# Graph network kernel, gated pass: the two edge-term columns made stationary, in four column groups

## What is computed

```
# layer 1: gated messages
msg_in = concatenate([h[src], h[dst], e64], axis=-1)
messages = (silu(msg_in @ w1 + b1) @ w2 + b2) * sigmoid(msg_in @ wg + bg)
agg = segment_sum(messages, dst) / max(deg, 1)
...
# layer 3, rounds 1 and 2: attention over edges
a_e = edge_attr_128 @ We @ att_e          # the edge term: one number an edge and round
alpha = leaky_relu(a_s[src] + a_d[dst] + a_e, 0.2)
```

## Time and profile before

| | us |
|---|---|
| median of 3 runs | 1996.36 |
| lowest, highest | 1994.1, 1997.79 |
| span of the profiled execution | 1993.2 |
| PE busy / weight loads busy | 1706.9 / 1412.5 |
| DVE / ACT / POOL busy | 1396.3 / 913.6 / 982.6 |

### The profile page before, as it was taken

The page is one execution under the profiler, slowest core; times in us unless marked ns, Lnnn a source line. Parts: engine busy times, 40 slices in busy tenths (PEclk is TensorE's granted clock), DMA queues, the critical chain, the costliest instruction groups (busy, mean ns, idle before and its releaser), DMA issues. The chain is left out here.

```text
span 1993.2 us, 43518 instructions
## 1 busy us (share of the span) xinstructions
PE 1706.9 (86%) x13678; PEld 1412.5 (71%) x13678; DVE 1396.3 (70%) x4290; ACT 913.6 (46%) x2490; POOL 982.6 (49%) x1002
## 2 busy tenths in 40 slices
PE   6799999999999749998649998956599989399996
PEld 5699999999998715556547886756478768166664
DVE  5677888888887698996667765556777654745556
ACT  2566676776776366773305553420255433411100
POOL 3766677777776120000557777735677774300000
PEclk9799999999999759999659999976699999699998
DMA  6887788888877002332532111117121111345442
GB/s 193 252 249 239 231 252 243 249 252 255 254 240 230 10 5 84 128 123 112 174 91 66 43 43 42 49 61 185 43 66 42 41 44 37 121 176 202 175 166 89
DMA packets 149677, 276.91 MB, mean 139 GB/s; under 512 B 28807, under 2 KB 88845, under 8 KB 147188
## 3 DMA queue, kind: packets, MB, share of 16 engines
q1 hardware_dynamic: 109134, 191.58, 29.5%
q0 software_dynamic: 35456, 79.88, 14.3%
q10 hardware_dynamic: 4854, 2.55, 0.5%
HBM read 228.82 MB, written 45.08 MB: 137 GB/s over the span
## 5 line engine op out<-in xcount | busy, mean ns | idle before, releaser
L972 POOL DMA_INDIRECT gated_rows<-p_tab,src_idx x416 | 429.0, 1031 | 176.4 <-issue 102.2
L1364 POOL DMA_INDIRECT ring<-table,src_idx x384 | 382.9, 997 | 145.3 <-issue 89.3
L2194 PE MATMUL bank<-counts,mean_xs 128*128 128x416 bf16 (+2 forms) x1350 | 220.1, 322 | 32.1 <-DVE mean_xs L1696 32.1
L1013 PE MATMUL bank<-gated_wide_q,gated_comb 128*128 128x256 f32 x832 | 218.6, 386 | 0.0
L1170 DVE TENSOR_TENSOR gated_pre<-bank,gated_rows 128x512 f32<-128x512 f32 x208 | 142.8, 687 | 105.1 <-PE bank L1013 103.0
L1496 ACT COPY attention_counts<-bank 128x475 f32 (+1 forms) x224 | 127.6, 570 | 183.7 <-PE bank L1523 179.9
L2194 PEld LDWEIGHTS bank<-counts,mean_xs 128*128 128x128 bf16 x1350 | 126.3, 98 | 116.6 <-issue 35.1
L1086 ACT ACTIVATE gated_sig<-gated_pre 128x512 f32<-128x512 f32 x208 | 131.2, 631 | 155.3 <-DVE gated_pre L1170 153.3
L1534 PE MATMUL bank<-attention_counts,h_sb 128*128 128x232 f32 (+1 forms) x900 | 193.3, 342 | 0.5 <-issue 0.5
L1534 PEld LDWEIGHTS bank<-attention_counts,h_sb 128*128 128x128 f32 x900 | 159.2, 192 | 28.3 <-issue 1.5
L1519 PE MATMUL bank<-attention_wide_a,scratch 128*128 128x300 f32 x448 | 161.1, 442 | 12.2 <-DVE scratch L1577 11.2
(11 more groups left out here) (440 smaller groups left out, 3985.9 us busy)
## 6 DMA issues: line engine op xcount, KB each, us to landing
counts<-count_tabs SPq DMA_DIRECT2D x16, 2675.0 KB, 9.9
h_sb<-in_edge_attr_dram SPq DMA_DIRECT2D x51, 512.0 KB, 4.9
count_tabs<-mean_counts SPq DMA_DIRECT2D x40, 535.0 KB, 2.7
gated_relr<-rel_rows SPq DMA_DIRECT2D x104, 128.0 KB
gated_ids<-id_rows SPq DMA_DIRECT2D x26, 512.0 KB
gated_wide_q<-q_tab SPq DMA_DIRECT2D x208, 64.0 KB
attend_hot_lo<-low_hots SPq DMA_DIRECT2D x52, 256.0 KB
gated_ea<-in_edge_attr_dram SPq DMA_DIRECT2D x51, 256.0 KB
```

The costliest lines, as they stand in the source:

```text
L972: pool.indirect_dma_start(out=rows[:, q % TICKS, c, :], out_offset=None, in_=p_tab, in_offset=bass.IndirectOffsetOnAxis(ap=src_idx[:, b, j ...
L1013: mm = pe.matmul(PRE[q % 2][:, c * 2 * P:(c + 1) * 2 * P], comb[:, u, k, c, :], wide_q[:, u, c, :], start=True, stop=True)
L1364: pool.indirect_dma_start(out=rows[:, n % RING, j, :], out_offset=None, in_=table, in_offset=bass.IndirectOffsetOnAxis(ap=src_idx[:, gathe ...
L2194: mm = pe.matmul(BANKS_D[q % ND][:, 0:width], xs[l][:, m // 3, m % 3, :], counts[:, s % 2, m // 3, at:at + width], start=(m == 0), stop=(m ...
```

## The change

The edge terms are made once a batch instead of once a step. `ae_v` becomes 32 columns wide, the last 30 of them zero, and is the stationary operand; the turned attributes of one chunk are the moving one, 128 columns. Each of the four chunks of a batch has its own group of 32 columns of the array: chunk j writes the PSUM partitions 32 j to 32 j + 31 of ST, and rows 32 j and 32 j + 1 are the two terms of its 128 edges, one row a round. The four products stand ahead of the silu transposes of the batch's second step (k = 1); the first step has none.

ACT copies the 128 x 128 result once a batch to `ae_rows`, ahead of the silu copy. SP stores rows l, 32 + l, 64 + l, 96 + l of four batches at a time in the DRAM tensor `edge_terms` (`keep_edge_terms`, two transfers for four batches). `attend` loads its round's rows with two transfers into `ae_jp`, and DVE rearranges them to `ae_e`; the transposes L2443 are gone. `place_eaT` waits for one more step of ST, since `eaT` is now read one step longer. Two semaphores for `ae_rows` and one for its placing are added to the 35 that the pass clears at its end.

```
+            ae_rows = sb("ae_rows", [P, 2, AG_, P])
...
+                    def keep_edge_terms(g):
+                        sp.wait_ge(ae_placed, (g + 1) * AG_)
+                        for l in range(2):
+                            sp.dma_start(edge_terms[l, g * AG_:(g + 1) * AG_, :, :].rearrange("b j p -> j b p"),
+                                         ae_rows[l:P:AE_COLS, g % 2, :, :]).then_inc(ae_kept[g % 2], 16)
...
+                            if b % AG_ == 0 and b >= 2 * AG_:
+                                keep_edge_terms(b // AG_ - 2)
...
                     def turn_silu(q):
                         pe.wait_ge(silu_ready, q + 1)
                         reach(pe, sT_ready, q)
+                        _, k, _ = batch(q)
+                        if k == PAIRS - 1:
+                            for j in range(J):
+                                pe.matmul(ST[j * AE_COLS:(j + 1) * AE_COLS, 2 * P:3 * P], ae_v[:, :], eaT[:, (q - k + j // 2) % TRN, j % 2, :],
+                                          start=True, stop=True, skip_group_check=True)
                         for c in range(2):
-                            pe.transpose(ST[:, c * P:(c + 1) * P], silu[:, q % 2, c, :], ident[:, :])
-                        for c in range(2):
-                            mm = pe.matmul(ST[:, 2 * (P + c):2 * (P + c) + 2], eaT[:, q % TRN, c, :], ae_v[:, :], start=True, stop=True)
+                            mm = pe.transpose(ST[:, c * P:(c + 1) * P], silu[:, q % 2, c, :], ident[:, :])
                         mm.then_inc(s_turned, 1)
...
-                        reach(act, s_turned, q - TRN + 1)
+                        reach(act, s_turned, q - TRN + 2)
...
-                        act.copy(ae[:, :, b, 2 * k:2 * k + 2], ST[:, 2 * P:2 * P + 4].rearrange("p (c l) -> p l c", l=2))
+                        if k == PAIRS - 1:
+                            reach(act, ae_kept[b // AG_ % 2], 32 * (b // AG_ // 2))
+                            act.copy(ae_rows[:, b // AG_ % 2, b % AG_, :], ST[:, 2 * P:3 * P]).then_inc(ae_placed, 1)
...
+                    even = NB // 16 * 16
+                    for rows_ in (slice(0, even), slice(even, NB)):
+                        sp.dma_start(ae_jp[rows_, :], edge_terms[l - 1, rows_, :, :].rearrange("b j p -> b (j p)")).then_inc(ae_loaded, 16)
...
-                        if g == AE_AT - 1:
-                            for j in range(J):
-                                mm = pe.transpose(A_SRC[0:NB, j * P:(j + 1) * P], ae[:, l - 1, :, j], ident[:, :])
-                            mm.then_inc(ae_turned, 1)
...
                         if g == AE_AT:
-                            dve.wait_ge(ae_turned, 1)
-                            link(dve.tensor_copy(ae_e[:, :].rearrange("b (p j) -> b j p", j=J), A_SRC[0:NB, :].rearrange("b (j p) -> b j p", p=P)))
+                            dve.wait_ge(ae_loaded, 32)
+                            link(dve.tensor_copy(ae_e[:, :].rearrange("b (p j) -> b j p", j=J), ae_jp[:, :].rearrange("b (j p) -> b j p", p=P)))
```

More of the change, by code:

```diff
@@ L163, in build_program @@
     place_a, origin_a = sb("place_a", [1, NSB * AROW], I32), sb("origin_a", [1, LAST], I32)
-    ae_v, ae = sb("ae_v", [P, 2]), sb("ae", [P, 2, NB, J])
+    AE_COLS = 32
+    ae_v = sb("ae_v", [P, AE_COLS])
     w_tab, w_c = sb("w_tab", [P, NB, J]), sb("w_c", [P, NB, J])
@@ L198, in build_program @@
     aux_rows = dram("aux_rows", [NB * BE, 4])
+    edge_terms = dram("edge_terms", [2, NB, J, P])
     tables = [dram(f"table{i}", [NODES, P]) for i in range(5)]
@@ L843, in gated_pass @@
             we_g, we_T, ae_c = sb("we_g", [P, 2, P]), sb("we_T", [P, 2, P]), sb("ae_c", [P, 2])
-            ae_in, ae_turned, ae_taken, ae_made = [sem(n) for n in ("ae_in", "ae_turned", "ae_taken", "ae_made")]
+            ae_in, ae_turned, ae_taken, ae_made, ae_blank = [sem(n) for n in ("ae_in", "ae_turned", "ae_taken", "ae_made", "ae_blank")]
+            AG_ = 4
+            ae_rows = sb("ae_rows", [P, 2, AG_, P])
+            ae_placed, ae_kept = sem("ae_placed"), [sem(f"ae_kept{i}") for i in range(2)]
             rows = sb("rows", [P, TICKS, 2, 2 * P])
@@ L867, in gated_pass @@
             SELF_AT = {16 + 8 * g: g for g in range(NG)}
-            per_round = [*self_sems, *ids_in, *looks_kept, looks_made, *ea64_in, *ea128_in, *relr_in, *q_in, ea_turned, made, s_turned, m_made, summed, eaT_ready, sig_ready, sT_ready,
+            per_round = [*self_sems, ae_placed, *ae_kept, *ids_in, *looks_kept, looks_made, *ea64_in, *ea128_in, *relr_in, *q_in, ea_turned, made, s_turned, m_made, summed, eaT_ready, sig_ready, sT_ready,
                          hot_b_ready, pre_ready, silu_ready, msg_ready, hot_ready, hotT_ready, added]
@@ L955, in _ @@
                             keep_looks(g)
+                        for g in range(NB // AG_ - 2, NB // AG_):
+                            keep_edge_terms(g)
+                        for u in range(2):
+                            sp.wait_ge(ae_kept[u], 32 * (NB // AG_ // 2))
                         for u in range(2):
@@ L1108, in _ @@
                     act.wait_ge(ae_made, 1)
-                    act.copy(ae_v[:, :], bank[7][:, 2 * P:4 * P:P]).then_inc(ae_taken, 1)
+                    act.wait_ge(ae_blank, 1)
+                    act.copy(ae_v[:, 0:2], bank[7][:, 2 * P:4 * P:P]).then_inc(ae_taken, 1)
                     with rounds_of(act) as rr:
@@ L1130, in _ @@
                     dve.memset(ones_b[:, :], 1.0).then_inc(ready, 1)
+                    dve.memset(ae_v[:, :], 0.0).then_inc(ae_blank, 1)
                     dve.wait_ge(loaded, 16 * 6)
@@ L2344, in attend @@
             scanned, carried, shifted, weighed, spare = sem("scanned"), sem("carried"), sem("shifted"), sem("weighed"), sem("spare")
-            ad_loaded, ae_turned = sem("ad_loaded"), sem("ae_turned")
+            ad_loaded, ae_loaded, ae_jp = sem("ad_loaded"), sem("ae_loaded"), sb("ae_jp", [NB, BE])
             scattered = kept_sem(f"attend{l}_scattered")
```

## The result

The changed kernel takes 1979.05 us (median of 4 runs, 1976.03 to 1981.16), the kernel before 1995.4 us (4 runs, 1994.1 to 1997.79): a ratio of 0.9916, 95% interval 0.9899 to 0.9932, or 16.3 us less. The forecast was 1979. But the trace says that it came out for other reasons than those given.

What follows compares the result with a forecast made beforehand. PE, dense in the gated pass, was taken to bound the kernel: -75.9 us removed, +57.2 added, +2 ACT waits, +0.5 last store, +0.2 semaphores, -0.9 in `attend`, together -17, hence 1979 us; range 1962 to 2016.

Steps and rivals of the forecast that it cites:

- What bounds the kernel: In the gated pass PE is dense at 2.81 us a step; POOL, at 2.49, takes over if a step falls over 0.32.
- rival 2: In a batch's edge terms all eight records run side by side: -43 us, 1953 us; chance 10%.
- Removed: In the gated pass PE loses the edge terms of each step, 0.365 us in 208 steps, 75.9 us.
- Added: In the gated pass PE gains four float32 products a batch, 0.55 us each batch, 57.2 us in all.
- chain of five intervals: In a batch's eight records, one product's second record runs beside the next product's first: 5 x 0.11 = 0.55 us.
- the third case: In a batch's edge terms the records run wholly side by side: two intervals, 0.22 us, taken as 0.24, 25 us in all.
- the one-column operands of the earlier trace ... going in costs nothing: On PE, switching from 128 columns to 32 and back was taken as free, from rows of one-column transposes.
- rival 3: At each switch of column width the array empties: 0.16 us, 0.32 a batch, 33 us; 2012 or 2045 us; chance 11%.
- The text's own test: Distance from L1040 to L1043 on PE: 0.55 us as forecast, 0.88 without overlap, 0.24 all side by side, over 0.85 with emptying.
- ACT: Behind the look-up tables, one step of eight, PE may wait up to 0.3 us for ACT's silu copy: 0 to 8, taken 2.
- The rest: Last store at the pass's end +0.5 us, three more semaphore clears +0.2, transposes gone from `attend` -0.9.
- rivals 1 and 3: Edge terms: column groups don't overlap (2012 us, 31%), or the array empties at each switch (2012 or 2045 us, 11%).

## Why the prediction was right in its number

**What bounds the kernel** held: PE leads, steps without terms take 2.453 us as forecast, and the others don't pass it as a whole. They are nearer than the text has them: POOL needs 2.67 us a step, not 2.49, since 0.30 us stand behind every gather. So rival 2's sum, which gave back 8 us for POOL at 2.57 us a step, is too fast: 0.10 x 208 = 21 us by these rows, an estimate.

**Removed**, 0.365 a step: the steps without terms went from 2.815 to 2.453, 0.362. Right.

**Added**, 0.55 a batch forecast, 0.504 measured, and this is two errors that cancel: the number is luck. The chain of five intervals doesn't exist: the records run in two waves, 0.22, which is the third case, given 10%. The chain took the records in issue order; the first records of all four products start within 20 ns. And the step "the one-column operands of the earlier trace rows ... going in costs nothing" failed: it read the price of a mode from transposes, and entering and leaving costs 0.28 a batch. A price at each switch is rival 3's, and near the size worked out for it (0.32). By the rows it is made up otherwise: 0.09 at each of the two switches where the text laid 0.16 bare, the rest in the start of the last wave and the transposes behind. That the array empties, as rival 3 says, and as "TensorEngine Tiling (Array Packing)" of the Trainium skill, Key Properties, has it with its drain, agrees with the holes, but no run shows what the loads wait for. Rival 2 and rival 3 together, which no case of the text combined, are what happened. The text's own test says it: it wanted 0.55 from L1040 to L1043 and the profile has 0.36, which is none of its cases.

**ACT**, 2 us taken out of 0 to 8: the mechanism was right, the place too (behind the look-up masks), the size was not. The step is 0.34 longer, in 18 of the 26 places: 5.8 us. The text took the slack of 0.16 against a step 0.2 to 0.4 shorter and came to up to 0.3, then took a quarter of it. The masks being spread took the wait away, which shows its origin.

**The rest**: end of the pass and clears 0.67 against 0.7, again the number and not the terms: the store, taken at 0.5, costs nothing, and the clears, taken at 0.2, cost all of it. `attend` -0.9: not resolved.

The sum with what was measured: 75.3 removed (0.362 x 208), 52.4 added (0.504 x 104), 5.8 of waits, 0.7 at the end: -16.4, and -16.3 measured, where the forecast had -75.9 + 57.2 + 2 + 0.7 - 0.9 = -17. The edge terms were 4.8 too dear, the waits 3.8 too cheap, and the gains of 75.9 and 0.9 together 1.5 too large.

The chances have a slip: rivals 1 and 3, both slower, were given 31 and 11%, which is 42 and not 39, and what stays within 0.2% is 4% and not 7.

## What to carry to other kernels

Float32 products with 32 stationary columns to four column groups are nearly free beside each other, but each visit to the narrow tiles costs 0.28 us between full-width work (shown for 32 columns in float32; no run has other widths or types): gather several products in one visit, and compare with the visit, not with the product. Then look at what the fewer visits lay bare: sixteen products at a time were 7 us slower than eight. Don't read the price of a tile size from transposes of that size. Where a step gets shorter, look for the engine that makes one long piece in every so many steps, and leave it some work to hide behind, or cut the piece up: a mean busy share of 0.82 hid a wait in one step of eight. And bound an engine by the distance of its starts where it waits for nobody, not by its busy time and the idle time that a view puts down to it alone.

## What the runs showed of the hardware

- Entering narrow tiles costs 0.09 us, leaving them 0.09 (0.12 with the staggered start of four records), and 0.055 more if float32 transposes come first behind them, 0.01 if it is the bf16 product L1049; nothing at full width with the same eight records. In both directions the first weight load begins 0.20 us after the start of the last record of 128 columns, with its product and not ahead of it.
- Inside a visit, records to different groups start 6 to 7 ns apart, the next wave 0.11 to 0.13 behind; the eight narrow loads had begun within 48 ns, the last four of them while the first four records, of the same groups, were running.
- A float32 transpose of 32 columns to the same rows, shown with the same tile 128*32, has none of these holes and takes 0.11 us.
- A gather of POOL that ran beside DVE's mask of 1.27 us lasted 2.29 us (18 of 18 from 150 to 560 us in the changed kernel), the others 0.97 on average; behind each gather stand 0.30 us in which POOL waits for nobody.
